# Causal attention on one core: the projections of q and v side by side, and the low part of xT ahead of an addition

## What is computed

```python
xn = _layernorm(x, axis=-1)
# _L0_attn_ref: B = 16, T = 512, H = 16 heads of dh = 64
q = (x @ Wq).reshape(B, T, H, dh).transpose(0, 2, 1, 3)
k = (x @ Wk).reshape(B, T, H, dh).transpose(0, 2, 1, 3)
v = (x @ Wv).reshape(B, T, H, dh).transpose(0, 2, 1, 3)
logits = jnp.einsum('bhqd,bhkd->bhqk', q, k)
logits = logits + causal[None, None] + _pos_bias(rel_pos_bias, T)[None]
logits = logits / dh
probs = jax.nn.softmax(logits, axis=-1)
out = jnp.einsum('bhqk,bhkd->bhqd', probs, v)
out = out.transpose(0, 2, 1, 3).reshape(B, T, H * dh)
return out @ Wo + bo
```

## Time and profile before

| | us |
|---|---|
| median of 3 runs | 2704.53 (2701.99 to 2706.19) |
| profiled execution | 2707.02 |
| its span, first to last instruction | 2705.2 |
| TensorE busy in the span | 2547.8 (94%) |
| ACT busy | 2158.3 (80%) |
| DVE busy | 2009.4 (74%) |
| POOL busy | 1629.7 (60%) |
| mean granted TensorE clock | 0.977 of full speed |

### The profile page before, as it was taken

One profiled execution on the slowest core, in us unless ns is written; L12 is line 12 of the kernel. 1 busy time (PEld: TensorE's weight loads), 2 busy tenths in 40 slices (PEclk: granted clock), 3 DMA queues, 4 the chain that ended last, 5 costly groups with the idle time before them and its releaser, 6 DMA issues. The chain is left out here.

```text
span 2705.2 us, 71234 instructions
## 1 busy us (share of the span) xinstructions
PE 2547.8 (94%) x24208; PEld 1988.1 (73%) x24208; DVE 2009.4 (74%) x5647; ACT 2158.3 (80%) x6335; POOL 1629.7 (60%) x1947
## 2 busy tenths in 40 slices
PE   7999999999999999999599999997979999999796
PEld 4777777777777777777378888885767888888575
DVE  4666666666666666666389999995659999999565
ACT  5888888888888888888389999996438999999642
POOL 3444444444444444444389999994229999999521
PEclk8999999999999999999799999998989999999898
DMA  2000000000000000000311111111111111111112
GB/s 72 7 7 10 9 9 5 8 7 9 9 9 5 10 7 7 9 6 5 103 41 41 38 42 39 38 42 46 33 26 40 38 42 42 38 40 42 46 33 79
DMA packets 128513, 77.07 MB, mean 28 GB/s; under 512 B 80196, under 2 KB 110736, under 8 KB 128144
## 3 DMA queue, kind: packets, MB, share of 16 engines
q1 hardware_dynamic: 127968, 72.34, 10.9%
q10 hardware_dynamic: 176, 0.07, 0.0%
HBM read 17.58 MB, written 8.41 MB: 10 GB/s over the span
## 5 line engine op out<-in xcount | busy, mean ns | idle before, releaser
L306 POOL TENSOR_SCALAR L<-L,rinv 128x128 f32<-128x128 f32 (+3 forms) x1024 | 522.4, 533 | 622.7 <-DVE rinv L488 622.7
L370 ACT ACTIVATE L<-L,nmax 128x384 f32<-128x384 f32 (+3 forms) x1024 | 571.8, 561 | 144.2 <-DVE nmax L474 144.2
L474 DVE CUSTOM_DVE_ANT_0 L<-bank,bias_tab 128x256 f32<-128x256 f32 (+3 forms) x1024 | 470.5, 479 | 180.3 <-PE bank L590 178.3
L886 ACT ACTIVATE f_L<-bank,f_nmax,f_rn 128x128 f32<-128x128 f32 x1024 | 459.9, 486 | 5.0 <-DVE f_nmax L1013 5.0
L863 POOL TENSOR_TENSOR f_rn<-f_ssq,f_mhalf 128x16 f32<-128x16 f32 x128 | 419.1, 3274 | 18.2 <-DVE f_ssq L997 4.7
L845 POOL TENSOR_TENSOR f_qkr<-f_ab 128x256 f32<-128x256 f32 x512 | 414.3, 838 | 10.3 <-DVE f_ab L964 10.3
L611 PE MATMUL bank<-ident,L 128*128 128x128 f32 x2560 | 370.4, 276 | 2.3 <-DVE PT L215 2.0
L611 PEld LDWEIGHTS bank<-ident,L 128*128 128x128 f32 x2560 | 296.8, 141 | 83.4 <-issue 46.1
L964 DVE TENSOR_TENSOR f_ab<-bank,f_tab 128x512 f32<-128x512 f32 x512 | 347.8, 680 | 8.8 <-ACT f_sq L876 8.8
L632 PE MATMUL bank<-PT,v 128*64 128x512 f32 (+3 forms) x2048 | 303.9, 439 | 0.6 <-DVE yacc L507 0.4
L632 PEld LDWEIGHTS bank<-PT,v 128*64 128x64 f32 x2048 | 126.8, 136 | 166.2 <-issue 164.9
(11 more groups left out here) (145 smaller groups left out, 6390.8 us busy)
## 6 DMA issues: line engine op xcount, KB each, us to landing
f_vm<-f_v SPq DMA_DIRECT2D x224, 128.0 KB, 2.4
f_hs<-xf SPq DMA_DIRECT2D x132, 32.0 KB
f_hs<-xf SPq DMA_DIRECT2D x132, 31.8 KB
xb<-in_L_attn_x SPq DMA_DIRECT2D x16, 256.0 KB, 2.8
out<-yacc SPq DMA_DIRECT2D x32, 128.0 KB, 1.8
f_hs<-xf SPq DMA_DIRECT2D x32, 128.0 KB
out<-f_acc SPq DMA_DIRECT2D x4, 1024.0 KB, 7.5
f_hs<-xf SPq DMA_DIRECT2D x32, 127.0 KB
```

The lines of the kernel that those rows point to most:

```text
L306: nc.gpsimd.tensor_scalar(t, t, rinv[:, h % RING, a, i:i + 1], 1.0, ALU.mult, ALU.mult).then_inc(s_N, 1)
L370: nc.scalar.activation(t, t, ACT.Exp, bias=nmax[:, ep % RING, a, i:i + 1], scale=-1.0, accum_out=rsum[:, ep % RING, a, i:i + 1]).then_inc( ...
L474: nc.vector.tensor_tensor_reduce(out=L[:, p % RING, a, LOFF[i]:LOFF[i] + (i + 1) * P], in0=ps_s[a][i], in1=bias_tab[:, 2 * p + a, T - (i + ...
L886: nc.scalar.activation(L[:, ot % 2, a, k, :], ps_s[a][:, k * P:k * P + P], ACT.Exp, bias=nmax[:, ot % 2, a, k:k + 1], scale=rn[:, ot % 2, ...
```

## The change

On TensorE the order of a slot becomes: transposes 0 and 1, projection of q, projection of v, transposes 2 and 3. On ACT fill 1 moves from behind `high` of q to ahead of the exponential (1,1). On DVE, in slot p == 4, `xT_low` moves from behind the addition to `yacc` to ahead of it. No instruction is added or removed, and no size changes.

```diff
@@ -374,10 +374,10 @@   (ACT)
                 exps(3, 1, lagging(b, p, par, 1))
                 if first:
                     table_out(3 * p + 2)
+                fills(1)
                 exps(1, 1)
                 if lead is not None:
                     high(lead, s_q, q_hi, s_qh, ps_o)
-                fills(1)
                 exps(2, 1)
                 if item is not None:
                     value_out(item)
@@ -496,6 +496,8 @@   (DVE)
                 fills(2)
                 logits(2, 0)
                 logits(3, 0)
+                if p == 4 and has_scores(b) and has_next(b):
+                    xT_low(b + 1, 1 - par)
                 if step is not None:
                     yb, j, ypar = step
...
                     nc.vector.tensor_tensor(yacc[:, half, :], ps_o[:, 0:2 * D].rearrange("p (t d) -> p t d", d=D), src,
                                             ALU.add).then_inc(s_Ya, 1)
-                if p == 4 and has_scores(b) and has_next(b):
-                    xT_low(b + 1, 1 - par)
                 logits(0, 0)
@@ -666,16 +666,16 @@   (TensorE)
                 transposes(0)
+                transposes(1)
                 if lead is not None:
                     pe.wait_ge(s_L, taken(b, p, 1, 0))
                     project(lead, wq_hi, wq_lo, s_q, ps_o)
-                transposes(1)
-                transposes(2)
                 if item is not None:
                     pe.wait_ge(s_L, taken(b, p, 1, 1))
                     if p == 6:
                         pe.wait_ge(s_XTl, at(b, 1, 2))
                     values_of(item)
+                transposes(2)
                 transposes(3)
```

## The result

| | before | changed |
|---|---|---|
| median | 2704.11 us (2701.99 to 2706.19, 4 runs) | 2748.45 us (2746.3 to 2751.15, 4 runs) |
| ratio, 95% interval | | 1.0162 (1.015 to 1.0174) |
| profiled execution | 2707.02 us, span 2705.2 | 2746.78 us, span 2744.9 |

The forecast was 2744.8 us in a range of 2735 to 2753. One more run of before than the three shown has moved its median by 0.4 us.

What follows compares the result with a forecast made beforehand. TensorE, busy 1240 of 1285 us, was taken to set the pace. Late y +43.9, p == 4 -5.4 and odd slots +1.8 gave +40.3 us: 2744.8 us on the median, range 2735 to 2753.

Steps and rivals of the forecast that it cites:

- TensorE's own work unchanged: TensorE's slot: transposes and projections take the same sum in either order, so grouping the projections saves 0 us.
- q_hi late by 0.75 us: ACT in steady slots: q_hi starts 0.74 us later, behind later transposes, fill 1 and the exponential (1,1).
- 0.41 us a slot: Steady slots: y's first weight load waits for late q_lo, 0.41 us in each of 107 slots, +43.9 us.
- The load is ahead of its product, so its lateness counts whole: At y on TensorE: the load, due 608.88, precedes its product at 608.99, so lateness counts from the load.
- The rival that counts from y's first product: No load ahead of its product: wait at y 0.31 us a slot, +29.6 us, 2734.1 us; 4 in 100.
- p == 4, -5.4 us: Slots p == 4: xT_lo goes before the yacc addition, k's projection starts 0.36 us earlier, 15 times, -5.4 us.
- a wait for xT_lo shorter by 0.3 to 0.4 us: Sign in slots p == 4: slots 0.3 to 0.4 us shorter, the wait for xT_lo shorter by as much.
- The margins behind q_lo: Steady slots after q_lo: fill 2 free by 0.3 us, yacc addition by 0.2, high part of k no new bound.
- The odd slots, +1.8 us: Third, fourth and second-last slots cost 0 to 0.74 us each, four closing slots little; +1.8 together, of 0 to 2.5.

Runs made afterwards that it cites:

- v alone earlier: Kernel before with xT_lo ahead of the yacc addition, plus v's projection moved ahead of transposes 2, q left in place: 2697.44 us, ratio 0.9975.
- fill 1 between: Changed kernel with fill 1 on ACT put between the exponential (1,1) and the high part of q: 2713.28 us, ratio 1.0038, steady slots 9.90 us.

## Why the prediction was right, and where its sizes were off

- *TensorE's own work unchanged:* right. In the changed slot everything from the first transposes to the last before y is back to back, and "v alone earlier" leaves the slot at 9.71.
- *q_hi late by 0.75 us:* right in mechanism and nearly in size. It was 2.11 - 1.39 = 0.72, made of 0.44 for TensorE's order and 0.28 for the exponential behind fill 1; with fill 1 between, q_hi came at 1.83. The run with fill 1 between and the one with the ACT edit undone (q_hi at 607.77 - 605.95 = 1.82) show the first part alone.
- *0.41 us a slot:* 10.18 - 9.72 = 0.46. The term that was mis-sized is the hand-over from q_lo to the load, taken as 0.05 from a place with a single wait. y has two waits, and the one for q_lo stood in the instruction ahead of the load; it took 0.12. The run with the waits swapped, with its 0.05, has slots of 10.11, so 0.07 in each of 107 slots, some 7 us, is this term; the medians differ by 6. The rest of the chain was reckoned 0.02 too long: 10.11 - 9.72 = 0.39, against the 0.41 forecast. The two errors partly cancel.
- *The load is ahead of its product, so its lateness counts whole:* right. The first load of y was 0.46 late, and the slot lost 0.46. The rival that counts from y's first product gave 0.31; in the run with the waits swapped, where the hand-over is the reckoned one, the slot lost 0.39. The Trainium skill ("TensorE: Matmul & The Clock Gate", Part 3, The mechanism) states that a weight load overlaps products in flight only when their row groups differ. This trace disagrees: in the kernel before the load at 608.88 overlaps a product of the same 128 rows. The opening of the same section also allows it for a load into the background weight buffer, and that no run here contradicts or shows.
- *p == 4, -5.4 us:* 15 x 0.36, right. xT_hi came 648.65 - 644.12 = 4.53 us behind the first transposes, 0.22 later than the 629.55 - 625.24 = 4.31 before (0.25 reckoned). Without a later ACT the same edit gives 0.58 (0.61 reckoned). As a sign the prediction named a wait for xT_lo shorter by 0.3 to 0.4 us; at the load it was 0.58, as v's wait took the difference.
- *The margins behind q_lo:* they held. No wait for fill 2, the addition or k_lo has appeared between TensorE's products in the steady slots. The weight loads' list of the changed kernel does name the addition ahead of the heads:

```profile
PEld bank L632 <- issue: 135.2, 555, 0.4
PEld bank L632 <- DVE yacc L509: 29.5, 80, 0.7
```

But those loads were idle as long before, 163.6 us put down to "issue" and 1.3 to the addition, against 164.7 now. The label has moved; no time was added.
- *The odd slots, +1.8 us:* right in size. The fourth slot went from 9.42 to 9.77, the second-last from 9.55 to 10.19, and the third is 11.31 against 10.84 in the DVE edit alone, whose first slots ran as fast as the changed kernel's. Together that is 1.5. The four closing slots took the same, 25.9 us from the last slot's start to the end of the last y.
- *Sum:* 107 x 0.46 - 15 x 0.36 + 1.5 = 49.2 - 5.4 + 1.5 = +45.3, against +44.3 on the medians. Taken straight from the profiled executions, the stretch from the fifth slot's start to the last slot's start grew from 1223.7 to 1267.6 us, by 43.9. The forecast was 40.3, so it was low by the hand-over's 7 us, less the 2 by which the rest of the chain was reckoned too long.
- *The profiled executions as a whole* differ by only 39.8. Two stretches that the change does not account for took less in the changed kernel: 0.8 us up to the fifth slot's start, in spite of two odd slots there, and 3.3 behind the last slot's start, where the transformer runs, the same in both. In both places the granted clock differed. Windows of 18 to 65 us, before and changed:

```profile
18.00:65.00 47.00, 38.73 (x218) 25.48 (x216) 22.11 (x86) 29.82 (x86) 18.78 (x34) 0.85 0.01 1
```

```profile
18.00:65.00 47.00, 37.49 (x227) 24.82 (x225) 23.25 (x89) 31.34 (x91) 19.23 (x34) 0.93 0.01 2
```

A clock of 0.85 means that TensorE had its lower level, 1.2 of 2.4 GHz, for three tenths of that stretch. From 60 to 100 us behind the last slot's start the clock was 0.90 before and 1.00 in the changed kernel; the DVE edit alone, with 0.92 there, took about as long behind the last slot's start as the kernel before (1416.9 and 1416.0 us, against 1412.7). That the clock is the cause of the 3.3 us is likely and not shown. A few us between two single executions say nothing about a change; the slots do.

## What to carry to other kernels

Where one engine has no wait left, a reordering on it can only lose, by what it delays elsewhere, so follow the moved result through every list that it passes, each in strict order: product, high copy, low copy, next load. An instruction that used to run in another engine's idle time is free only in that place; put behind something that is not ready, it lands on the path with whatever part of it is left when its follower could start (here 0.28 of about 0.49 us, 107 times). And what the full engine waits for should be served first by its neighbour, once it is ready: xT_lo was waited for when the addition was not, and putting it first is the useful third of this change.

## What the runs showed that I had not expected

- Of two waits of one TensorE instruction, the one that stands in a wait instruction of its own costs about 0.07 us more when it is the one that comes last: 0.12 against 0.05 from the end of DVE's write to the weight load, 10.18 against 10.11 us a slot. It held in all 107 and 108 slots of the two runs, and with it the wait that comes last is better carried by the load itself; other kinds of instruction were not tried.
- In that form the profile puts the load's idle time down to "issue" (46.7 us in the changed kernel), which reads like no wait at all.
- A weight load late by about 0.3 us cost 0.26 to 0.27 before transposes; before y all of the lateness, 0.46, was lost. Why they differ was not tried.
